# Preambles of two cross-attention stages, divided by halves of tokens and begun inside the experts' block

## The chip, the cores and the metric

The kernel runs on one core of one Trainium2 chip. The metric is the time of one execution on the device in microseconds (us). A core has TensorE (PE), VectorE (DVE), ScalarE (ACT), GpSimd (POOL) and SyncE (SP), each with its own instruction queue, and 16 DMA engines that they share. Engines work in order within themselves and wait for each other through semaphores.

## What is computed

A two-layer perceiver: cross attention to a context, self attention, a feed-forward block, and the same again with other variants. Cut to what the change touches:

```python
x = x + cross_attention(layernorm(x), ctx_1024, mask0, Wq, bq, Wkv, bkv, Wout, bout, 16)
x = x + self_attention_0(layernorm(x), ...)             # over the 16 samples at each position
x = x + experts(layernorm(x), w_router, w1, w2, bias)   # 8 experts, top 2, capacity 256
x = x + cross_attention(layernorm(x), ctx_1024, side, mask1, ...)
x = x + self_attention_1(layernorm(x), ...)
x = x + gated_fp4(layernorm(x), w_gate, w_up, w_down)   # weights and inputs quantized by blocks
```

x is 16 x 64 tokens of 256, the context 16 x 1024 of 256. In the experts each token takes its two best experts' rows, each times its weight, added to x.

## The kernel before

The kernel is a row of blocks. A block holds one stream of instructions for each engine; the next begins when all engines have ended theirs. After some blocks stands a block that only clears semaphores (`recycle_semaphores`). The 1024 tokens lie in x as 8 tiles of 128 x 256 (NT = 8); G = 2 halves of 128 features.

`start_block` (L1581) loads x, the identity and masks, computes two mask rows and stores them to memory. `cross_block` (L127) is a cross stage. Its loop (`batches`, L188) runs over 16 batches of 8 steps; a step takes two heads: scores (L381, TensorE), the maximum (L472, VectorE), exponentials (L583, ScalarE), reciprocal (L480), product with it (L647, GpSimd), turn (L394), two copies (L488, L592). Between these stand the projections of the next batch's keys and values (L327 to L329, in pieces of 512 columns and of 256 rows, three passes each) and the division of the context two batches on into a rounded part and a rest (`split_hi` L561 on ScalarE, `split_lo` L629 on GpSimd). The steps of each stream are written out by hand, so the order of the code is the order of the queues.

Ahead of the loop stands the preamble. SyncE loads queries' weights, keys' and values' weights, the first context, output weights, two bias rows (L266 to L276). VectorE takes the statistics of all 8 tiles (L504, L507) and normalizes them (L513) once GpSimd has taken the root (L651). TensorE turns the tiles (L423) and projects four query jobs (L429), job n being (feature half g, token half c); VectorE divides each into a rounded part and a rest (L520, L523, L525), SyncE stores them (L283, L284) and loads the first batch's queries back in another layout (`load_queries` L252), and GpSimd spreads them (`spread` L632). Context and weights are divided (L596, L561, L654, L629), the four key pieces and four value pieces of the first batch projected through two banks (`key_bank` L224), the keys' rests taken (`rest_key` L456), and SyncE moves them in 24 loads into a stacked form (`load_keys` L259).

`experts_block` (L1207) runs 8 experts; its result rows are scattered to memory (L1357), loaded back as rows taken by each token (L1242), and added to x with their weights (L1334, 16 additions). Between the experts' work it quantizes and turns the weights of the last stage, and stores them to memory (L1246 to L1251), from where they are loaded beside the last projection (L1721).

## Time and profile before

| | us |
|---|---|
| median of three runs (1445.78 to 1448.63) | 1445.81 |
| the profiled execution | 1448.41 |
| its span, first to last instruction | 1446.60 |
| TensorE busy in the span | 1265.4 (87%) |
| VectorE busy | 970.5 (67%) |
| ScalarE busy | 761.0 (53%) |
| GpSimd busy | 641.6 (44%) |

Busy shares are means over stages with different limits. The rows further below are lines of the timeline: start and length in us, engine, line of the kernel, operation, what it writes <- what it reads, how many of them stand together, and in brackets how long the engine was idle before and what ended that.

### The profile page before, as it was taken

To read this page: it belongs to the slowest core of one execution; us is meant where nothing else is said; L and a number is where in the kernel's file an instruction comes from.
4 is the path that set the end of the run, shared out by engine and by line. 5 is a ranking of instruction groups with operands and counts; after the bars stand their busy time and mean duration, and the time that the engine had idled before them with its cause. 6 is when DMAs were issued, how large, how long until landed. Compare 5 with 4: busy or idle time off the path is not lost. (4 is left out here: it accounts for less than half of the span.)

```text
span 1446.6 us, 34710 instructions
## 1 busy us (share of the span) xinstructions
PE 1265.4 (87%) x12182; PEld 1057.4 (73%) x12182; DVE 970.5 (67%) x1993; ACT 761.0 (53%) x1374; POOL 641.6 (44%) x576
## 2 busy tenths in 40 slices
PE   4899999999998787389965999999999997866687
PEld 2788888888886565378853888888888886545454
DVE  5577777777776555454425677777777775765696
ACT  2577777777775111021222777777777774232221
POOL 4456656566553132052314456566566653235000
PEclk9999999999999875579986999999999998968799
DMA  5877787777763431534536777777767762001000
GB/s 186 197 203 178 184 206 175 194 183 183 200 148 75 63 30 34 185 94 171 180 116 200 193 197 179 194 178 184 204 176 196 191 153 51 28 1 63 0 15 15
DMA packets 108371, 202.63 MB, mean 140 GB/s; under 512 B 43645, under 2 KB 65182, under 8 KB 108032
## 3 DMA queue, kind: packets, MB, share of 16 engines
q1 hardware_dynamic: 106752, 197.64, 53.4%
q0 software_dynamic: 1536, 3.88, 0.9%
q8 instruction: 53, 0.87, 0.3%
q14 instruction: 30, 0.25, 0.1%
HBM read 90.42 MB, written 12.78 MB: 71 GB/s over the span
## 5 line engine op out<-in xcount | busy, mean ns | idle before, releaser
L647 POOL TENSOR_SCALAR cross_prob<-cross_prob,cross_inverse 128x1024 f32<-128x1024 f32 x256 | 287.8, 1124 | 361.0 <-DVE cross_inverse L480 361.0
L583 ACT ACTIVATE cross_prob<-cross_negated,cross_negmax 128x1024 f32<-128x1024 f32 x256 | 294.9, 1152 | 131.4 <-DVE cross_negmax L472 130.9
L472 DVE CUSTOM_DVE_ANT_0 cross_negated<-cross_scores,cross_bias 128x1024 f32<-128x1024 f32 x256 | 313.5, 1225 | 30.1 <-PE cross_scores L381 12.5
L394 PE MATMUL cross_turn<-ident,cross_prob 128*128 128x128 f32 x2048 | 270.8, 275 | 11.8 <-POOL cross_prob L647 10.9
L394 PEld LDWEIGHTS cross_turn<-ident,cross_prob 128*128 128x128 f32 x2048 | 240.9, 142 | 50.9 <-POOL cross_prob L647 14.5
L592 ACT COPY cross_probT<-cross_turn 128x512 f32<-128x512 f32 x256 | 149.3, 583 | 66.2 <-PE cross_turn L394 65.1
L488 DVE COPY cross_probT<-cross_turn 128x512 f32<-128x512 f32 x256 | 175.6, 686 | 5.3 <-PE cross_turn L394 5.3
L629 POOL TENSOR_TENSOR cross_ctx_lo<-cross_raw,cross_ctx_hi 128x512 fp32r<-128x512 f32 x128 | 166.9, 1308 | 15.9 <-ACT cross_ctx_hi L561 15.9
L381 PE MATMUL cross_scores<-cross_keys,cross_qbd 96*128 96x512 f32 x512 | 168.4, 410 | 2.4 <-DMA cross_keys<-cross_key_hi 2.4
L327 PE MATMUL cross_out<-cross_wv_hi,cross_ctx_lo 128*128 128x256 f32 x496 | 150.4, 303 | 0.0
L329 PE MATMUL cross_out<-cross_wv_hi,cross_ctx_hi 128*128 128x256 f32 x496 | 139.7, 282 | 0.0
L328 PE MATMUL cross_out<-cross_wv_lo,cross_ctx_hi 128*128 128x256 f32 x496 | 139.3, 281 | 0.0
L480 DVE RECIPROCAL cross_inverse<-cross_total 128x1 f32<-128x1 f32 x256 | 42.0, 164 | 133.0 <-ACT cross_prob L583 131.8
L410 PE MATMUL cross_out<-cross_probT,cross_value 128*32 128x128 f32 x4096 | 127.8, 277 | 2.6 <-ACT cross_probT L592 1.8
L410 PEld LDWEIGHTS cross_out<-cross_probT,cross_value 128*32 128x32 f32 x4096 | 109.8, 111 | 26.4 <-issue 24.7
L327 PE MATMUL cross_proj<-cross_ctx_hi,cross_wk_lo 128*128 128x512 f32 x248 | 110.0, 444 | 6.2 <-DVE cross_key_lo L460 6.2
L328 PE MATMUL cross_proj<-cross_ctx_lo,cross_wk_hi 128*128 128x512 f32 x248 | 98.7, 398 | 0.0
L381 PEld LDWEIGHTS cross_scores<-cross_keys,cross_qbd 96*128 96x128 f32 x512 | 83.2, 189 | 21.0 <-issue 14.2
L329 PE MATMUL cross_proj<-cross_ctx_hi,cross_wk_hi 128*128 128x512 f32 x248 | 98.3, 396 | 0.0
L460 DVE SCALAR_TENSOR_TENSOR cross_key_lo<-cross_proj,cross_bk,cross_key_hi 128x512 fp32r<-128x512 f32 x124 | 92.0, 742 | 5.0 <-ACT cross_key_hi L569 4.9
L328 PEld LDWEIGHTS cross_out<-cross_wv_lo,cross_ctx_hi 128*128 128x128 f32 x496 | 94.2, 190 | 0.0
L327 PEld LDWEIGHTS cross_out<-cross_wv_hi,cross_ctx_lo 128*128 128x128 f32 x496 | 93.3, 188 | 0.2 <-DVE cross_key_lo L460 0.2
(236 smaller groups left out, 2009.8 us busy)
## 6 DMA issues: line engine op xcount, KB each, us to landing
cross_keys<-cross_key_hi SPq DMA_DIRECT2D x512, 128.0 KB, 2.4
cross_raw<-in_ctxT SPq DMA_DIRECT2D x32, 1024.0 KB, 5.7
cross_keys<-cross_key_lo SPq DMA_DIRECT2D x256, 128.0 KB, 2.4
cross_bias<-bias_rows SPq DMA_DIRECT2D x32, 512.0 KB, 3.7
up_sb<-in_moe_w SPq DMA_DIRECT2D x8, 1024.0 KB, 9.6
down_sb<-in_moe_w SPq DMA_DIRECT2D x8, 1024.0 KB, 11.8
cross_stacked_q<-q_rows SPq DMA_DIRECT2D x96, 64.0 KB, 2.1
q_rows<-cross_negated SPq DMA_DIRECT2D x8, 256.0 KB, 2.3
```

The lines of the kernel that those rows point to most:

```text
L327: pe.matmul(out, lhs[1], rhs[0], start=first, stop=False)
L328: pe.matmul(out, lhs[0], rhs[1], start=False, stop=False)
L329: return pe.matmul(out, lhs[0], rhs[0], start=False, stop=last)
L381: last = pe.matmul(ps_s[n % 2][:, at], qbd[par][:, n, :, :].rearrange("p h q -> p (h q)"), keys[:, n, at], start=True, stop=True)
L394: last = pe.transpose(ps_t[part][:, k * P:(k + 1) * P], prob[n % 2][:, kt * P:(kt + 1) * P], ident)
L410: last = pe.matmul(ps_o[32 * j:32 * j + 32, 0:P], value[par][:, kt, g * P + 32 * j:g * P + 32 * j + 32], probT[:, j, kt, :], start=(kt == ...
L472: dve.tensor_tensor_reduce(negated[n % 2][:, :], ps_s[n % 2][:, :], bias_sb[par][:, :], -1.0, 3.0e38, ALU.add, ALU.min, negmax[:, n % 2:n ...
L488: dve.tensor_copy(probT[:, j, 4:8, :], ps_t[1][:, :].rearrange("p (k q) -> p k q", k=4)).then_inc(turn_copied_v, 1)
L583: act.activation(prob[n % 2][:, :], negated[n % 2][:, :], ACT.Exp, bias=negmax[:, n % 2:n % 2 + 1], scale=-1.0, accum_out=total[:, n % 2:n ...
L592: act.copy(probT[:, j, 0:4, :], ps_t[0][:, :].rearrange("p (k q) -> p k q", k=4)).then_inc(turn_copied_a, 1)
L629: pool.tensor_tensor(ctx_lo[par][:, :, at], raw[:, :, at], ctx_hi[par][:, :, at].bitcast(F32), ALU.subtract).then_inc(lo_done, 1)
L647: pool.tensor_scalar(prob[n % 2][:, :], prob[n % 2][:, :], inverse[:, n % 2:n % 2 + 1], 1.0, ALU.mult, ALU.mult).then_inc(prob_ready, 1)
```

## The change

The cross stage's first context and its weights become an object `First` with its own loads and divisions, which can be issued by another block. For the first cross stage the opening block goes away: its loads, the mask rows and their store stand inside the cross block (`start`), x loaded in two halves. For the second, the loads are issued by SyncE behind the last expert's weights, ScalarE divides them between expert 6 and expert 7, and GpSimd takes the rests behind the scatter of expert 5. The additions of the experts' results to x move out of the experts' block into the second cross block (`taken`), interleaved with the statistics tile by tile; the rows taken are loaded into the buffers `value1` and `negated` of the cross stage.

Statistics, root, normalization, turns and query jobs go by halves of four tiles. Only the two jobs of the first half stand ahead of the loads of the first batch's queries; the last job's division stands in the loop's first batch, between its first and second maximum. The first batch's keys and values are projected through four banks. In the second stage SyncE moves the first batch's keys ahead of the query stores, in the first by feature halves between them. The output weights are loaded over the keys' weights (`load_out`). The quantized weights stay in on-chip buffers and are not stored and loaded. One more block that clears semaphores stands between self attention and the experts.

```diff
...
+class First:
+    def load_keys(self, sp):
+        for t, k in ((self.wk, "wk"), (self.wv, "wv")):
+            sp.dma_start(t[:, :, :], self.w[k]).then_inc(self.w_loaded, 16)
+        sp.dma_start(self.raw[:, :, :], self.ctxT[0].rearrange("(g p) k -> p g k", p=P)).then_inc(self.ctx_loaded, 16)
+    def load_out(self, sp):
+        sp.wait_ge(self.w_lo_done, 2)
+        sp.dma_start(self.wo[:, :, :], self.w["wo"]).then_inc(self.wo_loaded, 16)
...
+    def round_context(self, act):
+        act.wait_ge(self.ctx_loaded, 16)
+        for piece in range(4):
+            at = slice(piece * 256, (piece + 1) * 256)
+            act.copy(self.ctx_hi[:, :, at], self.raw[:, :, at]).then_inc(self.hi_done, 1)
...
+    def rest_of_context(self, pool, piece):
+        at = slice(piece * 256, (piece + 1) * 256)
+        pool.wait_ge(self.hi_done, piece + 1)
+        pool.tensor_tensor(self.ctx_lo[:, :, at], self.raw[:, :, at], self.ctx_hi[:, :, at].bitcast(F32), ALU.subtract
+                           ).then_inc(self.lo_done, 1)
...
+            def store_queries(n, stored):
+                (g, c), at = q_jobs[n], slice(q_jobs[n][1] * 512, q_jobs[n][1] * 512 + 512)
+                sp.wait_ge(q_step, 3 * n + 3)
+                sp.dma_start(q_rows[0, g * P:(g + 1) * P, at], q_hi(g, c)).then_inc(stored, 16)
+                sp.dma_start(q_rows[1, g * P:(g + 1) * P, at], q_lo(g, c)).then_inc(stored, 16)
+            def first_queries(g):
+                sp.wait_ge(first_q_stored[g], 32)
+                for part, source in enumerate((0, 0, 1)):
+                    sp.dma_start(stacked_q[32 * part:32 * part + 32, 4 * g:4 * g + 4, :],
+                                 q_rows[source].rearrange("(n r) t -> r n t", r=32)[:, 4 * g:4 * g + 4, 0:S]
+                                 ).then_inc(first_q_loaded[g], 16)
+            def first_keys(g):
+                sp.wait_ge(key_lo_done, 2 * g + 2)
+                for n in range(4 * g, 4 * g + 4):
+                    load_keys(n)
+            if start is not None:
+                for out, in_ in ((away[:, :], start["looked_away"]), (at_key[:, :], start["looked_at"]), (side, start["side"])):
+                    sp.dma_start(out, in_).then_inc(masks_loaded, 16)
+                first.load_keys(sp)
+                for h in range(2):
+                    sp.dma_start(x[:, 4 * h:4 * h + 4, :], start["x"].rearrange("(h i p) d -> h p i d", h=2, p=P)[h]
+                                 ).then_inc(x_loaded[h], 16)
+                sp.dma_start(ident, start["ident"]).then_inc(ident_loaded, 16)
+                sp.dma_start(half_mask[:, :], start["half_mask"]).then_inc(ident_loaded, 16)
+                first.load_queries(sp)
+                sp.wait_ge(masks_step, 3)
+                sp.dma_start(start["rows_out"][0], row0).then_inc(rows_stored, 16)
+                sp.dma_start(start["rows_out"][1], row1).then_inc(rows_stored, 16)
+                sp.wait_ge(rows_stored, 32)
             load_bias(0, 0)
             load_bias(1, 1)
             sp.wait_ge(lo_done, 4)
             load_ctx(1)
-            for c in range(T // 512):
-                sp.wait_ge(q_step, 3 * G * (c + 1))
-                at = slice(c * 512, (c + 1) * 512)
+            if taken is not None:
                 for g in range(G):
-                    sp.dma_start(q_rows[0, g * P:(g + 1) * P, at], q_hi(g, at)).then_inc(q_stored, 16)
-                    sp.dma_start(q_rows[1, g * P:(g + 1) * P, at], q_lo(g, at)).then_inc(q_stored, 16)
-                if c == 0:
-                    sp.wait_ge(q_stored, 32 * G)
-                    load_queries(0)
+                    first_keys(g)
+            for g in range(G):
+                store_queries(g, first_q_stored[g])
+            for g in range(G):
+                first_queries(g)
+                if taken is None:
+                    first_keys(g)
             sp.wait_ge(lo_done, 8)
             load_ctx(2)
-            for g in range(G):
-                sp.wait_ge(key_lo_done, 2 * g + 2)
-                for n in range(4 * g, 4 * g + 4):
-                    load_keys(n)
-            sp.wait_ge(q_stored, 32 * G * T // 512)
+            first.load_out(sp)
...
+            for n in range(G, len(q_jobs)):
+                store_queries(n, q_stored)
+            sp.wait_ge(q_stored, 32 * (len(q_jobs) - G))
...
+            project_key(0, 0, 0)
+            if start is not None:
+                pe.wait_ge(ident_loaded, 32)
+                pe.wait_ge(q_loaded, 32)
+                turn_tokens(0)
+                for n in range(G):
+                    project_queries(n)
+            for piece in range(1, 4):
                 project_key(0, 0, piece)
-            for piece in range(4):
+            for piece in range(2):
                 project_value(0, 0, piece)
-            pe.wait_ge(q_step, 3 * len(q_jobs))
+            if start is None:
+                turn_tokens(0)
+                for n in range(G):
+                    project_queries(n)
+            for piece in range(2, 4):
+                project_value(0, 0, piece)
+            turn_tokens(1)
+            for n in range(G, 2 * G):
+                project_queries(n)
...
+            def add_taken(i, k):
+                if k == 0:
+                    dve.wait_ge(taken["loaded"][i // 2], 32)
+                else:
+                    dve.wait_ge(added, 2 * i + 1)
+                dve.scalar_tensor_tensor(out=x[:, i, :], in0=first.home[k][:, i, :], scalar=taken["weight"][:, i, k:k + 1],
+                                         in1=x[:, i, :], op0=ALU.mult, op1=ALU.add).then_inc(added, 1)
+            def aggregate(i):
+                dve.wait_ge(seen, 2 * i + 1)
+                dve.bn_aggr(moments[:, i, :], stats[:, i, :]).then_inc(seen, 1)
+            def through(i):
+                if taken is not None:
+                    add_taken(i, 0)
+                if i % 4:
+                    note(i - 1)
+                if taken is not None:
+                    add_taken(i, 1)
+                if i % 4:
+                    aggregate(i - 1)
+                if i % 4 == 3:
+                    note(i)
+                    aggregate(i)
...
+            dve.memset(power[:, :], -0.5).then_inc(stat_step, 1)
+            for i in range(4):
+                through(i)
+            shift(0)
+            through(4)
+            normalize(0)
+            if start is not None:
+                for i in range(5, NT):
+                    through(i)
+                shift(1)
+                dve.wait_ge(rows_loaded, 48)
+                dve.wait_ge(q_loaded, 32)
+                rest_key(0, 0, 0)
+                dve.wait_ge(rows_stored, 32)
+                for n in range(G):
+                    split_queries(n)
+                for piece in range(1, 4):
+                    rest_key(0, 0, piece)
+            else:
+                dve.wait_ge(rows_loaded, 48)
+                dve.wait_ge(q_loaded, 32)
+                for i in range(5, NT):
+                    through(i)
+                    rest_key(0, 0, i - 5)
+                shift(1)
+                rest_key(0, 0, 3)
+                for n in range(G):
+                    split_queries(n)
+            normalize(1)
+            split_queries(G)
...
+                    if is_first(b) and n == 0:
+                        for g in range(G):
+                            dve.wait_ge(first_q_stored[g], 32)
                     maxima(b, par, n)
+                    if is_first(b) and n == 0:
+                        split_queries(G + 1)
...
+            if start is not None:
+                first.round_weights(act)
+                first.round_context(act)
+            act.wait_ge(rows_loaded, 48)
+            round_key(0, 0, 0)
+            if start is not None:
+                copy_tokens(0)
+            for piece in range(1, 4):
+                round_key(0, 0, piece)
+            for piece in range(2):
+                copy_value(0, 0, piece)
+            if start is None:
+                copy_tokens(0)
+            for piece in range(2, 4):
+                copy_value(0, 0, piece)
+            copy_tokens(1)
...
+            first.load_keys(sp)
+            first.load_queries(sp)
             for e in range(E):
                 sp.wait_ge(scattered[e], 16 * CT)
             for j in range(NT // 2):
                 for k in range(2):
-                    sp.dma_start(taken[k][:, 2 * j:2 * j + 2, :],
+                    sp.dma_start(first.home[k][:, 2 * j:2 * j + 2, :],
                                  results.rearrange("(k j i p) d -> k j p i d", k=2, i=2, p=P)[k, j]).then_inc(taken_loaded[j], 16)
...
+                if e == E - 2:
+                    first.round_weights(act)
+                    first.round_context(act)
...
-            for i in range(NT):
-                dve.wait_ge(taken_loaded[i // 2], 32)
-                for k in range(2):
-                    dve.wait_ge((biased, added)[k], i + 1 if k == 0 else 2 * i + 1)
-                    dve.scalar_tensor_tensor(out=x[:, i, :], in0=taken[k][:, i, :], scalar=weight[:, i, k:k + 1],
-                                             in1=x[:, i, :], op0=ALU.mult, op1=ALU.add).then_inc(added, 1)
-            dve.wait_ge(added, 2 * NT)
...
+                if e == E - 3:
+                    for n in range(2):
+                        first.rest_of_weights(pool, n)
+                    for piece in range(4):
+                        first.rest_of_context(pool, piece)
...
-        start_block(nc, "start", [(x[:, :, :], io["x"].rearrange("(i p) d -> p i d", p=P)), (eye, io["ident"]),
-                                  (half_mask[:, :], io["half_mask"])],
-                    io["looked_away"], io["looked_at"], io["side"], bias_rows)
-        cross(0)
+        with ExitStack() as own:
+            cross(0, first_of(0, own), {n: io[n] for n in ("x", "ident", "half_mask", "looked_away", "looked_at", "side")}
+                  | {"rows_out": bias_rows})
         recycle_semaphores(nc)
-        cross(1)
+        with ExitStack() as own:
+            first = first_of(1, own)
+            result = [own.enter_context(nc.sbuf_tensor(f"result{i}", [P, CAPACITY // P, D], F32)) for i in range(2)]
+            experts(lambda loads: add_turned_block(nc, "self0_add", oT, eye, x, moments, loads), first, result)
+            recycle_semaphores(nc)
+            cross(1, first, taken={"loaded": taken_loaded, "weight": weight})
...
```

GpSimd at the start of the first cross stage, before. `cross_rstd` is the root, `cross_ctx_lo` a rest of the context, `cross_qbd` the spread queries:

```order
L651 TENSOR_TENSOR cross_rstd<-cross_shifted,cross_power 128x8
L654 TENSOR_TENSOR cross_wk_lo<-cross_wk,cross_wk_hi 128x512
L654 TENSOR_TENSOR cross_wv_lo<-cross_wv,cross_wv_hi 128x512
L629 TENSOR_TENSOR cross_ctx_lo<-cross_raw,cross_ctx_hi 128x2x256 x8
L639 TENSOR_TENSOR cross_qbd<-cross_stacked_q,half_mask 96x512 x2
```

and after (L188 is the first context, L828 the second):

```order
L182 TENSOR_TENSOR cross_wk_lo<-cross_wk,cross_wk_hi 128x512
L188 TENSOR_TENSOR cross_ctx_lo<-cross_raw,cross_ctx_hi 128x2x256 x3
L855 TENSOR_TENSOR cross_rstd<-cross_shifted,cross_power 128x4
L188 TENSOR_TENSOR cross_ctx_lo<-cross_raw,cross_ctx_hi 128x2x256
L182 TENSOR_TENSOR cross_wv_lo<-cross_wv,cross_wv_hi 128x512
L855 TENSOR_TENSOR cross_rstd<-cross_shifted,cross_power 128x4
L828 TENSOR_TENSOR cross_ctx_lo<-cross_raw,cross_ctx_hi 128x2x256 x4
L840 TENSOR_TENSOR cross_qbd<-cross_stacked_q,half_mask 96x512 x2
```

The root stands behind three pieces of context and is taken in two halves, and the pieces of the second context follow the second root.

VectorE from the experts' additions into the second cross stage, before:

```order
L1334 SCALAR_TENSOR_TENSOR x<-experts_hidden,weight,x 128x256 x16
L1210 UNCONDITIONAL_BRANCH
L454 UNCONDITIONAL_BRANCH
L504 BN_STATS cross_stats<-x 128x6 x8
L507 BN_AGGR cross_moments<-cross_stats 128x2 x8
L509 MEMSET cross_power 128x8
L510 TENSOR_SCALAR cross_shifted<-cross_moments 128x8
L513 TENSOR_SCALAR cross_probT<-x,cross_moments,cross_rstd 128x256 x8
```

and after, from the first half's epsilon on (`cross_value` and `cross_negated` hold the rows taken):

```order
L657 TENSOR_SCALAR cross_shifted<-cross_moments 128x4
L631 SCALAR_TENSOR_TENSOR x<-cross_value,weight,x 128x256
L631 SCALAR_TENSOR_TENSOR x<-cross_negated,weight,x 128x256
L663 TENSOR_SCALAR cross_probT<-x,cross_moments,cross_rstd 128x256 x4
L631 SCALAR_TENSOR_TENSOR x<-cross_value,weight,x 128x256
L623 BN_STATS cross_stats<-x 128x6
L631 SCALAR_TENSOR_TENSOR x<-cross_negated,weight,x 128x256
L637 BN_AGGR cross_moments<-cross_stats 128x2
L575 SCALAR_TENSOR_TENSOR cross_key_lo<-cross_scores,cross_bk,cross_key_hi 128x512
```

The additions stand between statistics and a key's rest (L575), behind the first half's normalization.

SyncE in the second preamble, before, where the second pair of queries is stored and the keys follow:

```order
L255 DMA cross_stacked_q<-q_rows 32x8x64 x3
L283 DMA q_rows<-cross_negated 128x512
L284 DMA q_rows<-cross_probT 128x512
L283 DMA q_rows<-cross_negated 128x512
L284 DMA q_rows<-cross_probT 128x512
L245 DMA cross_raw<-in_ctxT 128x2x1024
L263 DMA cross_keys<-cross_key_hi 32x1024
L263 DMA cross_keys<-cross_key_lo 32x1024
```

and after, the last two of 24 key moves and what follows:

```order
L329 DMA cross_keys<-cross_key_lo 32x1024
L329 DMA cross_keys<-cross_key_hi 32x1024
L336 DMA q_rows<-cross_negated 128x512
L337 DMA q_rows<-cross_negated 128x512
L336 DMA q_rows<-cross_negated 128x512
L337 DMA q_rows<-cross_negated 128x512
L343 DMA cross_stacked_q<-q_rows 32x4x64 x6
L311 DMA cross_raw<-in_ctxT 128x2x1024
L163 DMA cross_wk<-in_cross_wo 128x2x256
L321 DMA cross_stacked_q<-q_rows 32x8x64 x3
```

The stores of the first half's queries stand behind all key moves, those of the second half (from `cross_value`) behind the loads of the first and second batch's queries.

## Rows read from the trace of the kernel before

**Rows 1.** Timeline (start, us, engine, operation xcount, [idle <-releaser]): first score steps, DVE

```profile
49.79 1.23 DVE L472 CUSTOM_DVE_ANT_0 cross_negated<-cross_scores,cross_bias 128x1024 f32<-128x1024 f32 x1 [7.18 <-PE cross_scores L381]
...
804.40 1.22 DVE L472 CUSTOM_DVE_ANT_0 cross_negated<-cross_scores,cross_bias 128x1024 f32<-128x1024 f32 x1 [5.34 <-PE cross_scores L381]
```

**Rows 2.** Timeline, first preamble, all engines

```profile
0.75 0.41 SPq L1602 DMA_DIRECT2D start_away<-in_looked_away  x1
9.46 2.71 DVE L504 BATCH_NORM_STATS2 cross_stats<-x 128x6 f32<-128x256 f32 x8 [3.10 <-PEq L1584]
11.38 0.47 SPq L245 DMA_DIRECT2D cross_raw<-in_ctxT  x1
14.82 4.57 DVE L513 TENSOR_SCALAR cross_probT<-x,cross_moments,cross_rstd 128x256 f32<-128x256 f32 x8 [1.76 <-POOL cross_rstd L651]
19.34 2.18 ACT L561 CAST cross_ctx_hi<-cross_raw 128x512 fp32r<-128x512 f32 x4 [3.55 <-DMA cross_raw<-in_ctxT]
20.03 4.95 POOL L629 TENSOR_TENSOR cross_ctx_lo<-cross_raw,cross_ctx_hi 128x512 fp32r<-128x512 f32 x4 [2.08 <-ACT cross_ctx_hi L561]
23.81 8.28 PE L429 MATMUL cross_scores<-cross_probT,cross_wq 128*128 128x512 f32 x16
27.06 0.75 DVE L520 TENSOR_SCALAR cross_prob<-cross_scores,cross_bq 128x512 f32<-128x512 f32 x1 [7.67 <-PE cross_scores L429]
29.04 0.75 DVE L520 TENSOR_SCALAR cross_prob<-cross_scores,cross_bq 128x512 f32<-128x512 f32 x1
...
41.14 0.69 ACT L569 ACTIVATE cross_key_hi<-cross_out,cross_bk 128x512 fp32r<-128x512 f32 x1 [0.72 <-PE cross_out L329]
...
44.43 0.59 ACT L574 COPY cross_value<-cross_out 128x512 f32<-128x512 f32 x1 [0.85 <-PE cross_out L329]
```

**Rows 3.** Timeline, experts' end up to the second cross stage

```profile
713.75 0.37 SPq L1237 DMA_DIRECT2D down_sb<-in_moe_w  x1
...
728.87 0.38 ACT L1302 ACTIVATE experts_hidden<-experts_h 128x256 f32<-128x256 f32 x1 [7.83 <-PE experts_h L1275]
...
746.84 4.17 SPq L1242 DMA_DIRECT2D experts_hidden<-results  x8
...
751.30 3.77 DVE L1334 SCALAR_TENSOR_TENSOR x<-experts_hidden,weight,x 128x256 f32<-128x256 f32 x8 [9.05 <-DMA experts_hidden<-results]
...
763.50 0.38 SPq L266 DMA_DIRECT2D cross_wq<-in_cross_wq  x1
```

**Rows 4.** Timeline, second preamble, queries and key moves

```profile
786.40 0.45 SPq L284 DMA_DIRECT2D q_rows<-cross_probT  x1
789.17 1.33 SPq L255 DMA_DIRECT2D cross_stacked_q<-q_rows  x3
792.58 2.04 POOL L639 TENSOR_TENSOR cross_qbd<-cross_stacked_q,half_mask 96x512 fp32r<-96x512 f32 x2 [1.91 <-DMA cross_stacked_q<-q_rows]
...
801.49 1.23 SPq L263 DMA_DIRECT2D cross_keys<-cross_key_hi  x2
803.53 1.09 PE L381 MATMUL cross_scores<-cross_keys,cross_qbd 96*128 96x512 f32 x4
```

**Rows 5.** Timeline, a block's end and the next start, semaphores cleared between

```profile
1322.84 0.37 ACT L1007 COPY oT<-self_att_o 128x256 f32<-128x256 f32 x1 [1.03 <-PE self_att_o L900]
1324.62 0.33 SPq L687 DMA_DIRECT2D gate_upT_sb<-gate_up_stored  x1
```

**Rows 6.** Timeline, start of two normalization blocks, the second behind late loads

```profile
1238.31 0.07 DVE L90 MEMSET self_norm_power<- 128x8 f32 x1 [0.57 <-PEq L677]
...
1334.62 0.07 DVE L90 MEMSET gated_norm_power<- 128x8 f32 x1 [1.22 <-PEq L677]
```

**Rows 7.** Windows: us, busy of five engines, PEclk, DMA share, GB/s

```profile
720.00:722.00 2.00, 2.00 (x13) 1.74 (x13) 0.69 (x1) 0.56 (x2) 0.00 (x0) 1.00 0.00 0
791.00:792.00 1.00, 0.00 (x0) 0.00 (x0) 0.96 (x3) 0.00 (x0) 0.00 (x0) 0.50 0.35 79
797.00:798.00 1.00, 1.00 (x7) 0.91 (x5) 0.00 (x0) 0.41 (x1) 0.00 (x0) 0.64 0.97 279
```

321 lines of the change are left out of this document (157 added, 164 removed).

## The prediction

> **What bounds the kernel now.** I read the windows first, then the timeline of each engine in the stretches that the change touches. TensorE is busy over most of the span, but each of the two cross stages is a loop of 16 batches with a preamble ahead of it, and a preamble is a chain of waits. The mark for its end is the first score step of VectorE (line 472): 49.79 us in the first cross stage and 804.40 in the second [rows 1]. From there on the instruction orders of before and after agree row by row on every engine, but for one query split, so the change is worth what it moves these two marks, plus small things at other places. The sum is made against the profiled execution, 1448.41 us (span 1446.60, 1.81 around it); the median of the three runs shown is 1445.81.
>
> **First preamble.** Before, a block of its own loads x and makes the mask rows; only then are the first context and the weights asked for, at 11.38, and ScalarE can divide the context from 19.34, 7.96 later [rows 2]. After, the order on SyncE is three mask loads, two weights, the context. SyncE issues one load in about 0.47, the first at 0.75 as before [rows 2], so the context is issued at about 3.1. It landed 7.96 after its issue when some 0.8 MB stood ahead and 1.4 MB behind it; now 0.6 MB stand ahead and x behind, so I keep 7.9: 11.0. Then, step by step:
> - GpSimd's rest of the context starts 0.69 after ScalarE (19.34 to 20.03) and takes 4.95 / 4 = 1.24 a piece [rows 2]. Three pieces: 11.7 + 3.7 = 15.4. The root, queued behind them, took up to 1.76 [rows 2]: 17.1. The statistics for it (four tiles, 2.71 / 8 = 0.34 each [rows 2], doubled for the waits between) are done by about 14.3 and are hidden.
> - Half of the normalization: 4.57 / 8 = 0.57 a tile [rows 2], as GpSimd works beside it: 19.4. Turn and copy, as an estimate 1.0: 20.4.
> - The first two query jobs: four jobs took 8.28, 2.07 each with the overlap of their ends [rows 2], 1.95 from start to start: 24.3. The first key piece was done while TensorE waited for the root. Three key pieces of 0.69 + 0.72 = 1.41 and four value pieces of 0.59 + 0.85 = 1.44 [rows 2] follow: 24.3 + 4.2 + 5.8 = 34.3.
> - Turn of the other half, 1.2, and its two copies, 0.7: 36.2. Only now ScalarE divides the second context, GpSimd follows by 0.7, four pieces at 1.24, up to 1.5 while VectorE splits queries beside it: 36.9 + 5.6 = 42.5. The spread of the queries is queued behind these, 2.04 / 2 = 1.02 [rows 4]: 43.5. Scores to first step took 804.40 - 803.53 = 0.87 [rows 1, 4]: **44.4**. TensorE has done its last query jobs at about 40, and is not what is late.
> The mark moves by 44.4 - 49.8 = **-5.4**. What is late afterwards is GpSimd, not TensorE or the queries' way through memory: their stores leave at about 25 and 27 and are back by about 31.
>
> **Last experts.** The division of the second stage's context and weights stands between expert 6 and 7 on ScalarE and behind expert 5's scatter on GpSimd, its loads behind the last expert weights on SyncE, issued at 713.75 [rows 3]. The DMA engines then have nothing to do: their share is 0.00 in 720 to 722 [rows 7]. Context issued at 713.75 + 0.37 + 2 x 0.47 = 715.1, landed by 723.0 with the 7.9 above, divided (2.18 [rows 2]) by 725.3. ScalarE's next real work, the first activation of expert 7, is wanted at 728.87 [rows 3]. So it costs nothing, with 3.6 to spare. GpSimd ends its six pieces at about 730 and its last scatter is wanted only after 742.
>
> **Second preamble.** Before, the eight loads of the experts' results are issued from 746.84 to 751.01, the additions run from 751.30, and the quantized weights are stored; the next block begins at 763.50, once all has landed [rows 3]. After, nothing holds the block but SyncE's issue: 751.0 plus a boundary with cleared semaphores, 1324.62 - 1323.21 = 1.41 [rows 5]: 752.5. Project keys at once; VectorE starts its chain:
> - A tile is two additions, statistics and an aggregate. An addition in a dependent row takes 3.77 / 8 = 0.47 [rows 3]; here they are interleaved, so I take 0.34 for each wide instruction and 0.1 for the aggregate: 1.1 a tile, and 1.4 as the upper bound. Four tiles and their tail: 757.6. Root 1.7: 759.4. Four normalizations, GpSimd being idle, nearer 0.34 than 0.57: 760.9. Two tiles and two key rests (0.67 each): 764.6, upper bound 767.
> - SyncE moves the keys now: 24 loads, two in 1.23 [rows 4], 0.635 each with the gap, so 15.3: 779.9. Behind them in its queue stand the stores of the queries. The queries are ready earlier: values 0 and 1, turn, two jobs at 1.95 give 771.7, and two splits of 29.04 - 27.06 = 1.98 [rows 2] give 773.9. They wait 6 us for SyncE.
> - Two stores 0.9, then 789.17 - 786.40 = 2.8 from the last store's issue to the issue of what waits for it, of which the last store's own landing is 2.3; I count 780.4 + 2.5 = 782.9 for the first pair. Three loads 1.33 and landing, 792.58 - 789.17 = 3.4 in all [rows 4]: 786.3. Spread 1.02, and 0.87: **788.2**.
> The mark moves by 788.2 - 804.4 = **-16.2**. The other chain, values, second turn, division of the next context and GpSimd's four pieces, ends at about 785, so it is 1 us behind the first.
>
> **Small things.** The last query split stands between the first and the second score step: three VectorE instructions, 1.98. The next step could begin 2.66 after the first, so this delays it by 0.7 in each loop if nothing absorbs it, by 0 if TensorE's slack does; I take 0.4 twice, **+0.8**. One more block that only clears semaphores stands between self attention and the experts: 1.41 - 0.57 [rows 5, 6] = **+0.8**. The last projection no longer loads the quantized weights: its successor started 1.22 after, against 0.57 without loads behind it [rows 6]: **-0.65**. The additions that left the experts' block are in the sum above, and so is the vanished boundary of the opening block.
> **Sum:** -5.4 - 16.2 + 0.8 + 0.8 - 0.65 = -20.6. On the profiled 1448.4 that is 1427.8; on the median 1445.8 it is **1425.2**.
>
> **Rivals.**
> - *TensorE at its lower clock in the second preamble.* In before the granted clock was 0.50 (1.2 GHz) in 791 to 792, when the array was idle, and still 0.50 to 797, though it worked again; it rose in 797 to 798 (0.64) [rows 7]. After, TensorE idles from its last turns to 752.5 and again before the value pieces. If everything after 762.7 ran at 1.2 GHz, value pieces and query jobs took up to twice 1.44 and 1.95, the last jobs would end at 793 to 796 and the mark would be at 794 to 797: a total of -12 to -15, 1431 to 1434. Against it: TensorE is nearly without a gap from 766 on, and in the rows five microseconds of work gave the clock back. The Trainium skill (TensorE: Matmul & The Clock Gate, Part 1) says that an array lately idle runs at half rate and a busy one at full rate, and asks for no long gaps between bursts of matmuls; by that rule, which the windows bear out, the key pieces at 752.5 run slow, which nothing waits for, and the rest is decided by the gap before the values.
> - *The key moves fill the DMA engines,* so that the query stores land behind them. Before, with keys and a 1 MB context under way together, their share was 0.97 [rows 7]. The two landings on the queries' way, some 2.4 each, cost 5 more at twice their length: 1430. Against it: the context has landed by 762, and 3.1 MB in 15.3 us is less than those engines moved then.
> - *More than I count.* A context that lands 1.5 earlier in the opening, a root of four columns at 0.9 instead of 1.7, no cost of the split: -20.6 - 1.5 - 0.8 - 0.8: 1422.
> - *Slower than before.* ScalarE waits for the second context in front of expert 7, and TensorE with it. It decides from a landing 11.5 us after the issue (726.7); each further microsecond costs one, and if TensorE's clock falls meanwhile the last expert's 14 us double. To lose all of 20.6 and 2.9 more, 1449, takes a landing 21 us after the issue, or 32 without the fall. Nothing in the trace lands so late, and the engines are free [rows 7].
> - *Nothing overlaps:* the additions or the key pieces wait for something that I read as ready (the taken rows, a bank), and the second mark moves only by the stores of the weights and the boundary, some 10 us: 1436.
>
> **How the numbers follow.** The forecast 0.63, the lower clock 0.12, the DMA engines 0.10, more than counted 0.08, nothing overlaps 0.05, slower 0.02. The range takes in the first four: upper bounds of the tiles (+2), of the queries' way (+6), and below -24. 1419.5 to 1433. A difference of 0.2%, 2.9 us, is about what can be told from none. Faster by more 0.96, same 0.02, slower 0.02.
>
> **What would show it.** In the profile of the changed kernel: first score steps at about 44.4 and 788; a first division of context at 11.0; expert 7's first activation at 729 with no wait for a load; the second cross block's first key piece near 752.5; SyncE issuing its 24 key moves without a gap from 764.6 and the query stores right behind; GpSimd the last before the first scores of the first stage; loops as long as before. I am wrong if the second mark is later than 791, or if the loops have another length.

## The result, and the profile after

| | before | after |
|---|---|---|
| median of 4 runs each, us | 1447.07 | 1434.32 |
| lowest to highest | 1445.78 to 1448.63 | 1433.95 to 1436.17 |
| ratio, 95% interval | | 0.9914 (0.9897 to 0.9931) |
| profiled execution's span | 1446.60 | 1432.40 |

The same pair measured twice more gave 0.9903 (0.9865 to 0.9940) and 0.9905 (0.9882 to 0.9928). The change is worth 13 to 15 us; 20.6 were forecast, and 1434.3 lies 1.3 above the range. The second preamble came out as worked out; the first gained a quarter to two thirds of what was forecast and gave 3.3 us back in its first batch.

Timeline of the changed kernel, first cross stage (start, length, engine, line, what it writes <- reads, in brackets the idle time before and what ended it); the mark is the row of L587, to be held against [rows 1]:

```profile
11.73 2.18 ACT L176 CAST cross_ctx_hi<-cross_raw 128x512 fp32r<-128x512 f32 x4 [4.80 <-DMA cross_raw<-in_ctxT]
17.29 3.27 DVE L663 TENSOR_SCALAR cross_probT<-x,cross_moments,cross_rstd 128x256 f32<-128x256 f32 x4 [1.12 <-POOL cross_rstd L855]
22.18 5.49 PE L530 MATMUL cross_scores<-cross_probT,cross_wq 128*128 128x512 f32 x8 [0.68 <-ACT cross_probT L789]
...
39.01 2.20 ACT L749 CAST cross_ctx_hi<-cross_raw 128x512 fp32r<-128x512 f32 x4
39.73 5.58 POOL L828 TENSOR_TENSOR cross_ctx_lo<-cross_raw,cross_ctx_hi 128x512 fp32r<-128x512 f32 x4 [15.73 <-ACT cross_ctx_hi L749]
45.27 2.03 POOL L840 TENSOR_TENSOR cross_qbd<-cross_stacked_q,half_mask 96x512 fp32r<-96x512 f32 x2
46.35 2.07 PE L476 MATMUL cross_scores<-cross_keys,cross_qbd 96*128 96x512 f32 x4 [3.46 <-POOL cross_qbd L840]
47.86 1.22 DVE L587 CUSTOM_DVE_ANT_0 cross_negated<-cross_scores,cross_bias 128x1024 f32<-128x1024 f32 x1 [3.67 <-PE cross_scores L476]
49.58 0.58 SPq L311 DMA_DIRECT2D cross_raw<-in_ctxT  x1
...
54.05 0.85 SPq L337 DMA_DIRECT2D q_rows<-cross_value  x1
55.13 0.62 ACT L749 CAST cross_ctx_hi<-cross_raw 128x512 fp32r<-128x512 f32 x1 [1.52 <-DMA cross_raw<-in_ctxT]
59.70 0.58 ACT L764 COPY cross_value<-cross_out 128x512 f32<-128x512 f32 x1 [1.24 <-DMA q_rows<-cross_value]
```

The chain to the mark is the forecast one: ScalarE's late division, GpSimd's four rests, the spread, the scores. What was not seen are the last two rows. ScalarE waits twice inside the first batch, for the third context and for the stores of the later queries. Both stand behind 24 key moves on SyncE. In the kernel before they stood ahead of them, and the same two ScalarE instructions waited for no transfer (timeline of SyncE, before):

```profile
37.20 0.36 SPq L283 DMA_DIRECT2D q_rows<-cross_negated  x1
...
39.07 0.56 SPq L245 DMA_DIRECT2D cross_raw<-in_ctxT  x1
39.68 0.70 SPq L263 DMA_DIRECT2D cross_keys<-cross_key_hi  x1
```

Timeline of the changed kernel, last experts and second preamble, to be held against [rows 3, 4]:

```profile
713.65 0.37 SPq L1445 DMA_DIRECT2D down_sb<-in_moe_w  x1
...
725.15 2.18 ACT L176 CAST cross_ctx_hi<-cross_raw 128x512 fp32r<-128x512 f32 x4 [2.72 <-DMA cross_raw<-in_ctxT]
728.78 0.38 ACT L1504 ACTIVATE experts_hidden<-experts_h 128x256 f32<-128x256 f32 x1 [1.45 <-PE experts_h L1477]
...
764.70 0.55 SPq L329 DMA_DIRECT2D cross_keys<-cross_key_hi  x1
...
779.91 0.58 SPq L336 DMA_DIRECT2D q_rows<-cross_negated  x1
...
785.90 1.03 POOL L840 TENSOR_TENSOR cross_qbd<-cross_stacked_q,half_mask 96x512 fp32r<-96x512 f32 x1 [2.02 <-DMA cross_stacked_q<-q_rows]
...
788.49 1.23 DVE L587 CUSTOM_DVE_ANT_0 cross_negated<-cross_scores,cross_bias 128x1024 f32<-128x1024 f32 x1 [5.72 <-PE cross_scores L476]
789.64 0.75 DVE L670 TENSOR_SCALAR cross_prob<-cross_out,cross_bq 128x512 f32<-128x512 f32 x1
```

Expert 7 waits for TensorE, not for the load (1.45). The key moves and query stores start within 0.1 of 764.6 and 779.9.

To see where the rest went I divided every profile at the same marks: first and ninth maxima of each cross stage, issue of the last expert weights, start of the gated normalization, last instruction of VectorE. The ninth maxima are the first step of the second batch, so the second and fifth columns are the lengths of a first batch. Lengths are in us, of one execution each; the runs below are in it too. The last column is the ratio of the run's time to that of the kernel before, measured beside it; its 95% interval reaches 0.0016 to 0.0042 either way.

| profile | to first maxima | to ninth | to last expert weights | to first, 2nd stage | to ninth | to gated | to end | ratio |
|---|---|---|---|---|---|---|---|---|
| before | 49.8 | 23.8 | 640.2 | 90.65 | 23.65 | 506.6 | 109.9 |  |
| before_again | 49.1 | 23.7 | 636.3 | 90.24 | 23.65 | 505.9 | 113.5 | 1.0006 |
| after | 47.9 | 27.0 | 638.8 | 74.84 | 24.19 | 507.5 | 110.1 | 0.9914 |
| again | 46.8 | 27.1 | 641.8 | 75.35 | 24.19 | 510.7 | 110.1 | 0.9903 |
| again2 | 46.2 | 27.3 | 635.0 | 74.94 | 24.18 | 507.5 | 110.1 | 0.9905 |
| split_ahead | 46.6 | 27.1 | 637.9 | 75.07 | 23.62 | 504.5 | 113.5 | 0.9909 |
| ctx2_sooner | 47.0 | 27.3 | 638.0 | 75.06 | 24.18 | 504.0 | 113.5 | 0.9926 |
| both_sooner | 47.4 | 25.3 | 637.3 | 74.98 | 24.18 | 507.4 | 110.1 | 0.9895 |
| ctx1_sooner | 43.0 | 33.7 | 638.5 | 75.44 | 25.72 | 505.4 | 113.5 | 0.9937 |
| act_queue | 48.5 | 27.1 | 639.6 | 75.58 | 23.73 | 507.5 | 110.1 | 0.9899 |
| engine_keys | 46.4 | 25.7 | 639.4 | 75.37 | 24.18 | 510.7 | 110.1 | 0.9885 |
| warm | 47.5 | 27.1 | 639.1 | 75.07 | 25.61 | 502.4 | 110.0 | 0.9905 |
| order1 | 47.6 | 27.5 | 636.1 | 72.30 | 26.84 | 510.6 | 110.1 | 0.9906 |
| no_overlap | 47.4 | 27.8 | 642.2 | 82.80 | 25.52 | 505.1 | 113.5 | 0.9961 |
| all_moves | 43.5 | 31.8 | 637.9 | 70.35 | 27.98 | 504.6 | 113.5 | 0.9898 |
| all_act | 43.0 | 30.1 | 639.5 | 68.92 | 25.86 | 506.8 | 108.1 | 0.9877 |
| all_keys | 42.3 | 24.5 | 639.0 | 70.32 | 24.96 | 504.5 | 113.5 | 0.9848 |

The columns with next to no work of the change in them (third, sixth, seventh) differ by up to 7, 8 and 5 us. A difference of two totals of single executions therefore tells nothing of a step under that. The other columns scatter less: the first mark stands at 46.2 to 47.9 in the three profiles of the changed kernel, the mark of the second stage at 74.8 to 75.4.

The fifth column takes two values where nothing in the second stage was edited: 24.2 in six profiles, 25.6 and 25.7 in warm and ctx1_sooner. They go with TensorE's clock. In the first it is back at 1.00 some 2 us behind the first maxima, in the two others only 8 us behind them. Windows of the same steps, after and then warm (columns: length, busy of PE, PEld, DVE, ACT, POOL, granted clock, DMA share, GB/s):

```profile
790.00:796.00 6.00, 4.46 (x29) 3.55 (x29) 4.59 (x10) 4.00 (x8) 2.51 (x3) 0.97 0.83 283
```

```profile
790.00:796.00 6.00, 5.35 (x19) 4.24 (x18) 4.59 (x10) 3.98 (x8) 2.25 (x3) 0.50 0.86 290
```

So a first batch that runs six microseconds longer at the lower level takes 1.4 to 1.5 us longer in these two profiles.

### The profile page after: what moved, and what is told of

It is laid out like the page before. It is cut to its first block and busy times, and to the rows that moved or that the text cites. A ratio compares the mean times of both kernels' runs of the same rounds, so it can differ in the third digit from the quotient of the medians.

```text
span 1432.4 us, 34726 instructions
## 1 busy us (share of the span) xinstructions
PE 1266.0 (88%) x12182; PEld 1058.1 (74%) x12182; DVE 966.8 (67%) x1995; ACT 760.8 (53%) x1374; POOL 641.2 (45%) x578
## 5 line engine op out<-in xcount | busy, mean ns | idle before, releaser
L587 DVE CUSTOM_DVE_ANT_0 cross_negated<-cross_scores,cross_bias 128x1024 f32<-128x1024 f32 x256 | 313.6, 1225 | 26.8 <-PE cross_scores L476 9.4
L828 POOL TENSOR_TENSOR cross_ctx_lo<-cross_raw,cross_ctx_hi 128x512 fp32r<-128x512 f32 x120 | 155.9, 1301 | 26.9 <-ACT cross_ctx_hi L749 26.9
L419 PE MATMUL cross_out<-cross_wv_hi,cross_ctx_lo 128*128 128x256 f32 x488 | 147.4, 302 | 0.0
L419 PE MATMUL cross_proj<-cross_ctx_hi,cross_wk_lo 128*128 128x512 f32 x244 | 107.1, 439 | 0.0
L421 PEld LDWEIGHTS cross_out<-cross_wv_hi,cross_ctx_hi 128*128 128x128 f32 x488 | 92.5, 190 | 0.0
```

The lines of the kernel that those rows point to most:

```text
L419: pe.matmul(out, lhs[1], rhs[0], start=first, stop=False)
L421: return pe.matmul(out, lhs[0], rhs[0], start=False, stop=last)
L587: dve.tensor_tensor_reduce(negated[n % 2], ps_s[n % 2][:, :], bias_sb[par][:, :], -1.0, 3.0e38, ALU.add, ALU.min, negmax[:, n % 2:n % 2 + ...
L828: pool.tensor_tensor(ctx_lo[par][:, :, at], raw[:, :, at], ctx_hi[par][:, :, at].bitcast(F32), ALU.subtract).then_inc(lo_done, 1)
```

## The experiments

**The same kernels again.**

> The changed kernel once more, nothing edited. It serves two purposes: a second profile, and a time beside the three variants below. First theory, that the 3.3 us lost between the end of the second cross stage and the gated stage come from TensorE's clock, which falls and rises in the second self-attention stage at other places from execution to execution: the marks of the two preambles stand where they stood (first maxima at 47.9 and 788.5, within 0.3), and the time from the last maxima of the second cross stage (1200.3) to the start of the gated normalization (1320.2), 119.9 us, may come out up to 3 us shorter, with a granted clock of 1.0 where it was 0.50. Rival, that something in the changed kernel itself makes this stretch longer than the 118.6 us of the kernel before: it comes out at 119.9 within 0.3 again.

> The kernel before once more, nothing edited, for a second profile of it. Its marks of the preambles should stand as in the first profile (49.8, and 90.65 us from the issue of the last expert weights to the first maxima of the second stage, both within 0.6). Theory, that the times from 1443.7 to 1456.0 of one and the same kernel come from TensorE's clock in the stretches without a full TensorE: the self-attention stages and the gated stage differ from the first profile by up to 3 us each, with matmul lengths that differ by the factor of two. Rival, that they come from the preambles' transfers: the marks differ by over 1 us.

> The changed kernel a third time, beside the two versions of this call. The preambles' marks as before (first maxima 46.6 to 47.9, ninth 27.0 to 27.1 later; 74.8 to 75.4 us from the last expert weights' issue to the second stage's first maxima, 24.19 to its ninth). By the theory that the rest of the scatter is TensorE's clock, the stretch from the second stage's last maxima to the end is 228 to 233 us with the self-attention and gated parts at one of a few lengths (95.2, 98.8 or 100.2; 110.1 or 113.5), as in the ten profiles so far; a length between these would speak against it.

In again and again2 the second mark came back within 0.5 us (75.35 and 74.94 for 74.84), the first at 46.8 and 46.2 for 47.9, further off than the 0.3 I gave. The kernel before came back within 0.7. The stretch from the last maxima of the second cross stage to the gated normalization was 119.9 in the first profile of the changed kernel, 123.0 and 119.8 in the others, 118.6 and 117.9 before: in again both what I said (up to 3 us shorter) and the rival (119.9) missed, since it can be longer too. That it takes only a few discrete lengths is not so: in all_act the self-attention part takes 97.6 and the last stretch 108.1, which fit none. What differs with the lengths is TensorE's clock. Windows of the same code in the second self-attention stage, before and after (columns: length, busy of PE, PEld, DVE, ACT, POOL, granted clock, DMA share, GB/s):

```profile
1297.00:1319.00 22.00, 15.12 (x460) 12.74 (x456) 16.55 (x18) 10.08 (x13) 13.98 (x12) 0.84 0.01 3
```

```profile
1281.00:1295.00 14.00, 13.00 (x284) 11.12 (x284) 10.62 (x11) 5.14 (x7) 7.12 (x8) 0.50 0.01 4
```

After, the array works for 13.00 of 14 us at 0.50 (1.2 GHz); before, the clock was 0.84 on average over these steps and the next ones. The fourth score step from the end, of 32 small matmuls, takes 1.15 before and 1.98 after (timeline, before and then after):

```profile
1295.95 1.15 PE L871 MATMUL self_att_s<-self_qkT,self_att_qbd 32*128 32x64 f32 x32
```

```profile
1278.76 1.98 PE L1081 MATMUL self_att_s<-self_qkT,self_att_qbd 32*128 32x64 f32 x32
```

From there to the gated normalization it is 38.7 us before and 41.4 after, 2.8 more, in code that the change leaves alone. Between the two profiles of the kernel before, the gated stage differs by 3.6 us in the same way: two windows of 20 us have 0.83 and 1.00 in one and 0.76 and 0.90 in the other. No run changed the clock alone in these stretches, so this is read from the traces and not shown by an experiment.

**What the last query split costs in the loop.**

```diff
             normalize(1)
             split_queries(G)
+            split_queries(G + 1)
...
-                    if is_first(b) and n == 0:
-                        split_queries(G + 1)
```

> Both cross stages: the division of the last query job stands ahead of the first maxima and not between the first and the second. Theory, that the three instructions in the loop cost 0.55 us where nothing else is late: in the second stage the ninth maxima come 23.65 us after the first (24.19 in the changed kernel, 23.65 in the kernel before), and the first maxima no later, since VectorE is idle for 5.7 us ahead of them. In the first stage the 27.0 to 27.1 us stay within 0.3, because its first batch is held by ScalarE's wait for the stores of the later queries (59.7), whose place in SyncE's queue is not changed. Rival, that TensorE's slack absorbs the split: 24.19 in the second stage as well.

Measured were 23.62 in the second stage and 27.05 in the first: the split costs 0.57 where nothing else is late and is hidden where something is. That is as expected.

**What holds the first stage's first batch.** Three runs moved the transfers it waits for.

```diff
                 for n in range(4 * g, 4 * g + 4):
                     load_keys(n)
+                    if taken is None and n == 5:
+                        sp.wait_ge(lo_done, 8)
+                        load_ctx(2)
...
-            sp.wait_ge(lo_done, 8)
-            load_ctx(2)
+            if taken is not None:
+                sp.wait_ge(lo_done, 8)
+                load_ctx(2)
```

> First cross stage only: SyncE issues the load of the third context in the middle of the second half of the key moves (behind the keys of pair 5) and not behind all 24 of them. Theory, that ScalarE's wait of 1.52 us for that load at 55.1 is SyncE's queue order: the load is issued near 46, lands near 52, the wait is gone, and the ninth maxima come 1.5 to 1.7 us earlier relative to the first (27.0 us between them becomes 25.4). Rival, that the DMA engines are the limit there (their share is 0.9 to 1.06 from 44 to 58): the load lands as late as before, at 55, or the keys come later by as much, and the 27.0 stay within 0.3. The time: 1.6 below that of the changed kernel by the theory, equal to it by the rival.

The wait for the context went, and nothing was gained: the distance was 27.3. The wait for the query stores took its place, 3.16 us instead of 1.24 (timeline, ScalarE, ctx2_sooner):

```profile
59.17 0.59 ACT L768 COPY cross_value<-cross_out 128x512 f32<-128x512 f32 x1 [3.16 <-DMA q_rows<-cross_value]
```

Then the stores too, right behind the last key move (the context as above):

```diff
-            sp.wait_ge(lo_done, 8)
-            load_ctx(2)
+            if taken is None:
+                for n in range(G, len(q_jobs)):
+                    store_queries(n, q_stored)
+            else:
+                sp.wait_ge(lo_done, 8)
+                load_ctx(2)
             first.load_out(sp)
             sp.wait_ge(qbd_ready, G)
             load_queries(1)
-            for n in range(G, len(q_jobs)):
-                store_queries(n, q_stored)
+            if taken is not None:
+                for n in range(G, len(q_jobs)):
+                    store_queries(n, q_stored)
```

> First cross stage only: SyncE issues the third context's load behind the keys of pair 5, as in the run ctx2_sooner, and the stores of the last two query jobs right behind the last key move, ahead of the output weights and the second batch's queries. In ctx2_sooner the wait for the context was gone and the one for the stores had grown from 1.24 to 3.16 us. Theory, that the first batch is held by whatever stands last in that one queue: with both moved the ninth maxima come 24.2 to 24.8 us after the first (27.0 to 27.3 so far), and the stores, issued at about 49.5 and 51.0, are back by 55. Rival, that the DMA engines are full there (0.9 to 1.17 from 44 to 58) and every transfer lands when the sum of them is done: 27.0 stays within 0.4, with another wait in the place of these two.

The distance came to 25.3, between theory and rival: half of the 3.3 is back, with 1.23 us still waited for the same stores. So the order of the queue is one part. The next run gives those transfers a queue of their own (SyncE's part, which leaves them out of its queue, is not shown, nor is the last query split put ahead of the loop):

```diff
             for piece in range(4):
                 split_hi(1, 1, piece)
+            if taken is None:
+                for n in range(G, len(q_jobs)):
...
+                    act.dma_start(q_rows[0, g * P:(g + 1) * P, at], q_hi(g, c)).then_inc(q_stored, 16)
+                    act.dma_start(q_rows[1, g * P:(g + 1) * P, at], q_lo(g, c)).then_inc(q_stored, 16)
+                    if n == G:
+                        act.wait_ge(lo_done, 8)
+                        act.dma_start(raw[:, :, :], ctxT[2].rearrange("(g p) k -> p g k", p=P)).then_inc(ctx_loaded, 16)
```

> First cross stage only, with the last query split ahead of the first maxima as in split_ahead: the third context's load and the stores of the later query jobs are issued by ScalarE, which is idle there, on its own queue, while SyncE issues its key moves. This tells SyncE's issue rate (0.635 us a move, one after the other) from the DMA engines as the limit of the first batch; moving the same transfers forward within SyncE's queue gave 25.3 and 31.8 us between first and ninth maxima where 23.7 would be without a wait. Theory, that the one queue is the limit: stores issued at about 43 and 45.5, the context at 45, all landed before 52, 23.6 to 24.0 us from first to ninth maxima. Rival, that the DMA engines are: the stores and the context land no earlier than the key moves around them, the first maxima stay, and the distance stays above 25. The other stretches as in the changed kernel.

The rival held, with 27.1. The context was issued at 46.25, 3.3 earlier, on an idle queue, and ScalarE still waited for it until 55.71, while single key moves took SyncE 1.27 and 1.65 to issue instead of 0.59 (timeline, act_queue):

```profile
46.25 0.59 ACTq L820 DMA_DIRECT2D cross_raw<-in_ctxT  x1
...
55.71 0.62 ACT L750 CAST cross_ctx_hi<-cross_raw 128x512 fp32r<-128x512 f32 x1 [2.06 <-DMA cross_raw<-in_ctxT]
```

So SyncE's issue rate is not the limit. The sum of the DMA share over 26 to 62 us (18 windows, each share times 2 us) is 25.6 in the changed kernel, and 25.2 to 26.2 in the six other orders of the same 7.0 MB that the table has; in all of them the share falls to nothing between 57 and 60.

Full DMA engines are not enough for a cause, though. In the kernel before the same sum is 28.2, in its second profile 28.6, and the engines are busy to 60 as well (window, before):

```profile
38.00:58.00 20.00, 17.46 (x103) 14.96 (x104) 7.65 (x15) 9.24 (x16) 5.55 (x5) 0.91 1.03 260
```

Its first batch took 23.8 all the same, since the context and the stores stood ahead of the key moves. To test the amount of transfers as the other part, a third of the key moves was taken off the DMA engines:

```diff
+        def third_part(copy, n):
+            g, j = n // 4, n % 4
+            copy(keys[64:96, n, :], key_hi[32 * j:32 * j + 32, g, :].bitcast(F32)).then_inc(keys_loaded[n], 16)
...
-                for part, source in enumerate((key_hi, key_lo, key_hi)):
+                for part, source in enumerate((key_hi, key_lo) if first_batch and taken is None else (key_hi, key_lo, key_hi)):
...
             normalize(1)
+            if start is not None:
+                for n in range(4):
+                    third_part(dve.tensor_copy, n)
```

(and pairs 4 to 7 by ScalarE behind the second context's division.)

> First cross stage, first batch only: of the three moves that each head pair's keys need, the third (the rounded keys once more, to partitions 64 to 95) is a copy by VectorE (pairs 0 to 3, in its idle time from 34.6) or by ScalarE (pairs 4 to 7, from 41.2) and no longer a transfer. Nothing is left out. Theory, that the DMA engines are the limit: their busy time from 26 to 62 us falls from 25.5 to about 20.7, it ends at 53 to 54, SyncE's last store of the later queries is issued near 50, the waits of ScalarE for the context and these stores shrink to under 0.5 us each, and the ninth maxima come 23.9 to 24.6 us after the first (27.0 to 27.3), 71 to 72. Rival, that something in the first batch itself, not a transfer, costs the 3 us: the distance stays above 26.5.

The sum fell to 20.8, the last busy window is 52 to 54, and both waits for transfers are gone. The ninth maxima came 25.7 after the first, not the 23.9 to 24.6 of the theory. What is left is the clock, 0.50 from 46 to 54 and a wait for the scores in its place (windows, then timeline, engine_keys):

```profile
50.00:52.00 2.00, 1.34 (x6) 0.91 (x6) 0.91 (x2) 1.05 (x1) 1.03 (x1) 0.50 1.04 395
52.00:54.00 2.00, 2.00 (x11) 2.00 (x11) 1.78 (x4) 2.00 (x6) 1.45 (x2) 0.50 0.21 81
```

```profile
55.95 1.23 DVE L592 CUSTOM_DVE_ANT_0 cross_negated<-cross_scores,cross_bias 128x1024 f32<-128x1024 f32 x1 [0.86 <-PE cross_scores L481]
```

The theory holds for the waits. For the whole 3 us it holds only together with the clock: with the 1.4 that such a stretch cost in the second stage taken off, 25.7 becomes 24.3 (an estimate). In length the run is no better than both_sooner, which kept all transfers.

**The first mark by itself.** ScalarE divides the second context at once, in its idle time:

```diff
             if start is not None:
                 copy_tokens(0)
+                for piece in range(4):
+                    split_hi(1, 1, piece)
...
-            for piece in range(4):
-                split_hi(1, 1, piece)
+            if start is None:
+                for piece in range(4):
+                    split_hi(1, 1, piece)
```

> First cross stage only: ScalarE divides the second context right behind the first two turned token tiles, in time it spent idle (22.1 to 29.1), so that GpSimd can take its four rests before the queries are back. SyncE's order is untouched. Theory, that the spread behind the four rests on GpSimd is what the first scores wait for (39.7 to 46.3 us): the first maxima are then bound by TensorE's last query job, which ends at 42.9, and come at about 44, 3.6 to 3.9 us earlier. The third context, whose load stands behind the key moves on SyncE, is issued at 49.6 as before, so ScalarE's wait for it grows by nearly the same amount, from 1.5 to about 5, and the ninth maxima and the time gain less than 1 us. Rival, that the first scores wait for the queries' way through memory or the keys: the first maxima stay at 47.9 within 0.5. Second rival, that the gain at the mark is kept: the ninth maxima and the time move by 3.6.

The first maxima came at 43.0, so GpSimd's rests did hold the mark. But the first batch grew to 33.7, and the ninth maxima came at 76.7 instead of 73.5 to 74.9. The time was 1439.2 (0.9937, 0.9921 to 0.9953) beside 1435.8 for the changed kernel; the intervals overlap. I had expected the gain to be eaten but for less than 1 us; it was more than eaten, with 7.37 us of waiting for the third context (timeline, ctx1_sooner):

```profile
43.04 1.23 DVE L587 CUSTOM_DVE_ANT_0 cross_negated<-cross_scores,cross_bias 128x1024 f32<-128x1024 f32 x1 [0.49 <-PE cross_scores L476]
...
56.88 0.62 ACT L749 CAST cross_ctx_hi<-cross_raw 128x512 fp32r<-128x512 f32 x1 [7.37 <-DMA cross_raw<-in_ctxT]
```

**The second mark by itself.**

```diff
             if taken is not None:
-                for g in range(G):
-                    first_keys(g)
+                first_keys(0)
...
                 first_queries(g)
-                if taken is None:
+                if taken is None or g == 1:
                     first_keys(g)
```

> Second cross stage only: the two stores of the first half's queries and both loads of the first batch's queries stand between the keys of the first four pairs and those of the last four, not behind all 24 key moves. Theory of the prediction, that the queries are ready at 774 and wait 6 us for SyncE: the stores are issued at 773 to 776, the first batch's queries at about 778.5, and they are back near 781.5. What is late next is GpSimd, whose four rests of the second context end at 783.9 with the spread behind them: first maxima at 786 to 786.5, 2.0 to 2.5 us earlier than 788.5. Rival, that the stores are slow by themselves or that GpSimd's chain already binds: the mark stays at 788.5 within 0.4. Rival two, that the key moves of the second half, now ending near 784.5 to 786, make the later steps of the first batch wait: the mark moves but the ninth maxima (812.7) do not.

The mark came 2.5 to 3.1 earlier (72.3), so the queries did wait for SyncE, and the first batch took 26.8 instead of 24.2: the sum of the two, 99.1, is that of the changed kernel (99.0 to 99.5). The second rival held, only with another waiter than it named: the third context and not the keys (timeline, order1):

```profile
783.49 1.23 DVE L586 CUSTOM_DVE_ANT_0 cross_negated<-cross_scores,cross_bias 128x1024 f32<-128x1024 f32 x1 [3.17 <-PE cross_scores L475]
...
791.41 0.62 ACT L748 CAST cross_ctx_hi<-cross_raw 128x512 fp32r<-128x512 f32 x1 [2.18 <-DMA cross_raw<-in_ctxT]
```

**What the division inside the experts is worth.** In the second stage, loads and divisions were put back into the cross block (the experts' part for ScalarE is shown, GpSimd's rests moved with it):

```diff
+            if taken is not None:
+                first.load_keys(sp)
+                first.load_queries(sp)
             load_bias(0, 0)
...
-                if e == E - 2:
-                    first.round_weights(act)
-                    first.round_context(act)
...
```

> Second cross stage only: loads and division of its first context and of its weights stand in the cross block itself again, and not inside the experts' block; everything else is as in the changed kernel. Theory of the prediction, that the early division is what lets the keys be projected at once: context landed at about 759.5, its rests at 765, SyncE's key moves begin at about 768.5 and not at 764.7, the first maxima come 78.9 to 80 us after the issue of the last expert weights (74.8 to 75.4 so far), 4 to 5 us later. The stretch of the experts itself stays as it was. Rival, that the queries' chain alone sets the mark: it moves by less than 1 us.

The mark came at 82.8 instead of 74.8 to 75.4, so the division inside the experts is worth 7.5 to 8, more than the 4 to 5 I gave. The time rose with it, to 1444.9 (0.9961, 0.9941 to 0.9981). Measured from the issue of the last expert weights, the context landed 3.1 later than I had it: beside the weights and bias rows it took 8.4 from its issue (timeline, no_overlap), near the 7.9 that the prediction had used elsewhere:

```profile
757.87 0.46 SPq L151 DMA_DIRECT2D cross_raw<-in_ctxT  x1
...
766.23 2.18 ACT L176 CAST cross_ctx_hi<-cross_raw 128x512 fp32r<-128x512 f32 x4 [3.15 <-DMA cross_raw<-in_ctxT]
```

**TensorE kept busy ahead of its first work.**

```diff
+            if start is not None:
+                pe.wait_ge(warm_set, 1)
+                for i in range(36):
+                    pe.matmul(ps_o[:, :], warm[:, 0:P], warm[:, :], start=True, stop=True)
             project_key(0, 0, 0)
...
```

> First cross stage only: ahead of its first key piece, while it has nothing to do until 15.1, TensorE works off 36 matmuls of 512 columns on zeros that nothing reads; an added piece of work, nothing left out. In the changed kernel the first key piece's matmuls and the first five of the eight of the first two query jobs follow each other at twice the time of the later ones (0.43 for 0.23, 0.85 for 0.43), although the clock column says 1.00 in 12 to 26. Theory, that this is TensorE at its lower level after idling, and a term of 2 us that the prediction left out: with the array busy before, the key piece's matmuls follow at 0.23, the two query jobs end 2.0 us sooner (25.7 for 27.7 at the same start), and the first maxima and the ninth come 1.5 to 2 us earlier, 45.0 to 45.9 and 72 to 73. Rival, that the doubling comes from the operands just written by other engines: the spacing stays, the marks too.

The marks did not move beyond their scatter (first maxima at 47.5, the ninth 27.1 later). The first matmuls of the key piece followed each other at 0.23 to 0.30, the later ones at 0.38 to 0.42 again, and the two query jobs took 5.63, against 5.49 in the changed kernel (timeline and windows, warm):

```profile
14.89 0.40 PE L421 MATMUL cross_scores<-cross_ctx_lo,cross_wk_hi 128*128 128x512 f32 x1
15.13 0.40 PE L422 MATMUL cross_scores<-cross_ctx_hi,cross_wk_hi 128*128 128x512 f32 x1
...
15.74 0.63 PE L421 MATMUL cross_scores<-cross_ctx_lo,cross_wk_hi 128*128 128x512 f32 x1
16.16 0.63 PE L422 MATMUL cross_scores<-cross_ctx_hi,cross_wk_hi 128*128 128x512 f32 x1
```

```profile
14.00:16.00 2.00, 1.41 (x5) 1.22 (x6) 1.61 (x5) 0.00 (x0) 1.89 (x3) 0.85 0.18 53
16.00:18.00 2.00, 0.79 (x2) 0.07 (x1) 1.17 (x1) 0.69 (x1) 2.00 (x3) 0.50 0.37 135
```

At the slower spacing the column now reads 0.50, so the doubling is the lower level and not the operands. It was not lifted by work that ends at 11.7: the array idles from there to 14.6 and again while the tiles are normalized. What the full rate would be worth to the mark stays unmeasured. The rule that the prediction took from the Trainium skill (TensorE: Matmul & The Clock Gate, Part 1), that an array lately idle runs at half rate, agrees with the spacing here; the prediction had weighed it for the second preamble and left it out of the first.

**Versions that go for the whole.** The first, all_moves, has the early division and SyncE's order made for the loop (its part on SyncE is shown). The second, all_act, loads the second half of the first batch's queries and the third context through ScalarE's queue, and has the matmuls of warm. The third, all_keys, adds the copies of engine_keys in both stages and leaves those matmuls out.

```diff
-            for g in range(G):
-                first_queries(g)
-                if taken is None:
-                    first_keys(g)
+            first_queries(0)
+            if taken is None:
+                first_keys(0)
+            first_queries(1)
             sp.wait_ge(lo_done, 8)
             load_ctx(2)
+            sp.wait_ge(key_lo_done, 4)
+            for n in range(4, 8):
+                load_keys(n)
+                if n >= 6:
+                    store_queries(n - 4, q_stored)
...
```

> Both cross stages: the second context divided by ScalarE behind the turned tiles (first stage) or the rounded keys (second), and SyncE's order made for the loop: first queries' stores and loads behind the keys of pairs 0 to 3 (second stage) or ahead of them (first), third context right behind these, ahead of the keys of pairs 4 to 7, the later queries' stores between and behind those. Theory, that a mark can be moved to keep only if the third context and the stores move with it: first maxima at 43.0 in the first stage as in ctx1_sooner, the ninth 24.2 to 25 later (33.7 there), so 67.5 in place of 74; in the second stage first maxima 69 us after the last expert weights' issue (74.8 to 75.4 so far), the ninth 24.2 to 25 later. In all 10 to 13 us off the changed kernel, near 1423. Rival, that the DMA engines or SyncE's issue of 24 key moves, at 0.635 us each, are the limit: what is gained at the marks is lost again in the first batch, 26.8 or more in both stages, and the time gains under 4 us.

> Both cross stages: as all_moves (second context divided early, queries ahead of the keys of pairs 4 to 7), but the second half of the first batch's queries and the third context are loaded by ScalarE's queue behind its last copies, and TensorE has the 36 matmuls on zeros of the run warm. Theory, that SyncE's queue is the limit: first maxima at 41.5 to 43, the ninth 24.2 to 26 later; in the second stage first maxima 68 to 69.5 us after the last expert weights' issue, the ninth 24.2 to 26 later; the time 8 to 12 us below the changed kernel's. Rival, that the transfers themselves fill the DMA engines (24 key moves of 128 KB keep them at 0.92): the ninth maxima come at 72 or later in the first stage and 97 or later after that issue in the second, and the gain stays under 5 us.

> Both cross stages as all_act (second context divided early, queries of the first half ahead, later queries and third context on ScalarE's queue) without the matmuls on zeros, and the third part of the first batch's keys copied by VectorE and ScalarE as in engine_keys, in the second stage all eight pairs by ScalarE. Theory, DMA engines as the limit: first maxima at 42.5 to 44, ninth at 69 to 70.5 in the first stage (73.1 in all_act); in the second stage the ninth come 91 to 93 us after the issue of the last expert weights (94.8 in all_act, 99.0 to 99.5 in the changed kernel). In all 10 to 12 us off the changed kernel run beside it. Rival, that the earlier transfers were only ScalarE's or VectorE's slack in another form: the copies delay splits and values, and the ninth maxima stay at 73 and 95.

| | median, us | ratio to before (95%) | ninth maxima, 1st stage | from last expert weights to ninth, 2nd |
|---|---|---|---|---|
| changed kernel, measured beside all_keys | 1433.6 | 0.9905 (0.9882 to 0.9928) | 73.5 | 99.1 |
| all_moves | 1433.7 | 0.9898 (0.9868 to 0.9928) | 75.3 | 98.3 |
| all_act | 1430.0 | 0.9877 (0.9845 to 0.9908) | 73.1 | 94.8 |
| all_keys | 1425.7 | 0.9848 (0.9827 to 0.9870) | 66.8 | 95.3 |

In all_moves the marks moved nearly as far as wanted (43.5 and 70.35 for 43.0 and 69) and the ninth maxima did not: its rival held. In all_act ScalarE waited 4.59 us for the query stores until 56.51, with the DMA share at 0.92 to 1.08 from 38 to 56. So its rival held in the first stage; in the second the theory did, and 4.3 us were gained (94.8 for 99.1). With a third of the key moves gone, all_keys kept the gain: its ninth maxima came at 66.8, its longest wait for a transfer there is 0.39, and its time is 8 us below the changed kernel, where I gave 10 to 12, with intervals that do not meet. Its clock column reads 1.00 from 26 to 62 us, that of all_act 0.50 to 0.65 in 48 to 52 and 58 to 62, so part of the 6.3 us between their ninth maxima may be the clock's. In its second stage the 95.3 are no better than all_act's, against my 91 to 93: there the copies brought nothing.

## Why the prediction was right in parts and wrong in sum

- **First preamble, forecast -5.4, measured -1.9 (profile), -3.0 and -3.6 in the two others against the same 49.79, each 0.7 less against the second profile of the kernel before.** The chain was right, each link late by a little. Context 11.73 for 11.0; four normalizations 3.27 for 2.28, beside a GpSimd at work; first query job at 22.18 for 20.4; two jobs 4.9 to the next matmul for 3.9 and scores to first step 1.51 for 0.87, both at TensorE's lower level. The row for the jobs [rows 2] is of four jobs, most of whose matmuls follow each other at the full rate; the two that count here have five of their eight at half of it. The first three links give 1.8 at 22.18, the jobs 1.0 more, the scores 0.6.
- **The sentence that failed** is "From there on the instruction orders of before and after agree row by row on every engine, but for one query split, so the change is worth what it moves these two marks". SyncE's orders do not agree. The third context was issued at 39.07 ahead of the key moves in the kernel before, and at 49.58 behind them and behind the mark after; the later queries' stores at 37.20 to 38.57 before and at 52.58 to 54.05 after. The first batch took 27.0 us instead of 23.8: 3.25 more, where the sum had 0.4 for the query split and nothing for waits. The waits for the two transfers are 1.52 and 1.24. SyncE's queue was followed up to the mark and not beyond it. The runs bear this out: with both moved forward half came back (both_sooner), with fewer key moves both waits went (engine_keys).
- **The key moves fill the DMA engines** was a rival at 0.10, placed in the second preamble. There it did nothing to the mark (stores issued at 779.91, first queries spread at 785.90). Its reason against was wrong all the same: it counted bytes, and the key moves held the share at 0.88 to 0.94 with only some 200 GB/s from 766 to 778. In the first stage full engines are part of what holds the first batch: in engine_keys, with fewer moves, the waits were gone. They are not the whole, since the kernel before had them as full and lost nothing.
- **TensorE at its lower clock** was a rival at 0.12 in the second preamble. It came true in part and cost nothing at the mark: the clock read 0.50 in 764 to 766 and 0.87 in 766 to 768, the first two splits ended at 775.2 instead of 773.9, and their stores waited for SyncE until 779.91. Where it did cost was the first preamble, in which the prediction gave it no place.
- **Last experts, forecast free of charge.** Right: the context was divided from 725.15 and not 723.0, of the 3.6 to spare 1.45 were left. It landed 10.0 after its issue and not 7.9, which brings the slower rival nearer than I gave it. That rival's own sum has a slip: without the fall of the clock, 1449 takes a landing 35 us after the issue, not 32.
- **Second preamble, forecast -16.2, measured -15.8** (90.65 to 74.84), by every step named: first key move 764.70 (764.6), last store's turn 779.91 (779.9), maxima 788.49 (788.2, on the old start). In the last links two misses nearly cancel: the spread began 0.4 earlier than forecast, and from the scores to the first step it took 1.50 and not 0.87. That SyncE bound the mark is shown by order1, and that this other order bought nothing at the ninth maxima, too; all_act, with other queues and an earlier division, did gain 4.3 there.
- **Split, +0.54 to 0.57** (0.4), in the second stage only. **The block more that clears semaphores** costs 0.80 by the idle time of the first instruction behind it, 1.78 before and 2.58 after; the gated normalization starts after 0.57 and not the 1.22 in [rows 6], -0.65 as forecast (timeline, before and then after):

```profile
574.52 0.85 DVE L1078 TENSOR_TENSOR x<-x,self_add_b 128x256 f32<-128x256 f32 x2 [1.78 <-PE self_add_b L1071]
```

```profile
574.95 0.85 DVE L1288 TENSOR_TENSOR x<-x,self_add_b 128x256 f32<-128x256 f32 x2 [2.58 <-PE self_add_b L1281]
...
1320.20 0.07 DVE L90 MEMSET gated_norm_power<- 128x8 f32 x1 [0.57 <-PEq L887]
```

- **The sum.** -20.6, plus 3.5 at the first mark, plus 2.85 in its first batch, is -14.25; the profiles differ by -14.2. That they agree so well is luck: against what the forecast has for them, the other stretches are off by -2.2 (to the last expert weights), +0.4, +0.1, +1.6 (to the gated normalization) and +0.2, which nearly cancel. In the forecast time there is 1.3 more: with one run more the median of before was 1447.07 and not 1445.81. The range took its upper end from single mechanisms and none from this scatter, which the spread of the runs of before (2.85) already hinted at.

Not settled is what makes one execution spend more of the self-attention stage at 0.50 than another, and how the 3.25 of the first batch divide between the order of the queue, the amount of transfers and the clock.

## What to carry to other kernels

A mark inside a pipeline is worth what it moves only if every transfer that the next round needs moves with it: list what is issued behind the step that you put forward, and follow it to its first user. Where several orders end at the same time, add up the DMA engines' busy time over the stretch, in the kernel before as well: here moving forward what is waited for gave back half, and with fewer transfers the waits went. Cost TensorE's first work after a pause at the level that the pause leaves, and price the scatter of stretches that the change doesn't touch into the range.

## What the runs showed of the hardware

- Moves of 128 KB within the on-chip memory, to 32 partitions each, kept the DMA engines at 0.88 to 0.95 with some 200 GB/s (one every 0.635 us); where context loads and query stores were under way a share of 1.0 to 1.06 gave up to 404 in windows of 2 us. A copy of such a piece took 1.04 us on ScalarE, and 0.69 (engine_keys) to 0.88 (all_keys) on VectorE.
- A context load of 1 MB was back 5.0 to 10.0 us after its issue in the changed kernel, 5.6 as the median; it took 9.5 on a queue of its own, issued among key moves (act_queue).
- The clock column read 1.00 from 12 to 26 us in the changed kernel while its matmuls followed each other at the slower spacing (0.43 for 0.23). In the kernel before it read 1.00 as well while the first query matmuls followed each other at 0.85 and the later ones at 0.43. In these openings the spacing tells the level and the column doesn't.
- One kernel, unchanged, took from 1441.0 to 1456.0 us in the runs of before. TensorE can be busy and stay at the lower level: for 93% of 14 us at 0.50 in the changed kernel (1281 to 1295), and in the kernel before for 92% of 40 us (522 to 562).
